# Attention and a mixture of experts on one core: the router's choice through PSUM, a small DMA descriptor memory, and a new order of work on every engine

## The chip, the cores and the metric

The kernel runs on one core of a Trainium2 chip. Five engines share the core's on-chip memory and run their own instruction streams: PE (TensorE, matmuls), DVE (VectorE), ACT (ScalarE), POOL (GpSimd) and SP (SyncE, which here only issues DMA transfers). The metric is the device time of one execution in microseconds; less is better.

## The reference, cut to what matters

```python
x = x + _L0_xattn_ref(_layernorm(x), ctx_1024, ctx_1024)     # x, ctx_1024: (16, 256, 256) f32: 4096 tokens of 256
x = x + _L0_ffn_ref(_layernorm(x), gate_w, gate_b, w1, b1, w2, b2)

# attention within one token: its 16 heads (16 values each) attend to the 16 heads of the same token of ctx
qh, kh, vh = [z.reshape(B, S, 16, 16) for z in (q, k, v)]
scores = jnp.einsum('bsqd,bskd->bsqk', qh, kh) / 4, causal over the heads
out = jnp.einsum('bsqk,bskd->bsqd', softmax(scores), vh)

# router and experts: 8 experts, each token goes to the one with the largest logit
top1 = jnp.argmax(xf @ gate_w.T + gate_b, axis=-1)
for e in range(8):
    h = relu(xf @ w1[e].T + b1[e])        # 256 -> 1024
    y = h @ w2[e].T + b2[e]               # 1024 -> 256
    out = out + jnp.where((top1 == e)[:, None], y, 0)
```

## The kernel before, in words

**Attention** goes in 16 chunks of 256 tokens (`NC`, in the code `i`). Of each chunk the queries are normalized on DVE (L974, L977, with the mean and deviation spread over the partitions by a PE product with `sel`, L1387), and queries, keys and values are split into a high and a low f16 half: the high one on ACT (L786, L794, L802), the rest on POOL (L1282, L1289, L1296). Small DMAs lay queries and values out as block diagonals in `arena` (L601, L603, L607; five of eight from SP's queue, three from ACT's). PE then makes the scores (L1396 the mask and L1403, 96 small products), DVE, ACT and POOL the softmax (L985 to L1000, L849, L1304), PE turns it (L1420) and multiplies by the values (L1433, 96 products), and DVE adds the residual (L1012).

**The router** works on groups of 4 chunks (`NG` = 4 groups, `g`). PE turns the group's output (L1445, in four steps) and makes the logits in the PSUM bank `lg_ps` (L1459, in four steps of four heads, 8 matmul rows each); DVE normalizes (L1020 to L1030, POOL's power L1321 between) and chooses: the generator `choose` in L1033 to L1094 is a chain of 15 small DVE steps per group that ends with `slot_i`, each row's place in a list sorted by expert. POOL then scatters the group's rows to DRAM (`sorted_rows`, L1340, 8 indirect DMAs). Three stages of a plan (L1113 to L1179) say which tile of 128 sorted rows belongs to which expert. The first 9 tiles need groups 0 and 1, the next 8 also group 2, the last 22 all four.

**The experts** work on 39 tiles of 128 rows: SP fetches a tile (L747), ACT and DVE normalize and split it (L871, L877, L1193), a DMA turns it (L767), PE makes the hidden layer (`ups`, L1506, 8 steps of 6 products), DVE, ACT and DVE its bias, relu and split (L1203, L886, L1214), PE the second layer (`downs`, L1522 and L1523, 8 steps of 2 products), DVE the result (L1228) and POOL stores it by an indirect DMA (L1366). The weights of the 8 experts are loaded (L660, L672, L679, L685) and split on ACT (L863) and DVE (L1186) while attention runs; the last of them land after it.

**The order.** On each engine the work is a set of generators, one for each kind of step. `weave` merges them by the table `TIMES`: every step has a number there, and an engine issues its steps in the order of these numbers. Nothing waits for a number; only their order counts, and each engine works strictly in that order, SP's DMA issues too. What an instruction needs is guarded by semaphore waits in front of it.

## Time and profile before

| | before |
|---|---|
| median of 3 runs | 467.47 us (467.33 to 468.16) |
| span of the profiled execution, first to last instruction | 462.9 us |
| what lies around the span, by the median | 4.6 us |
| PE busy | 384.6 us, 83% |
| DVE busy | 339.8 us, 73% |
| POOL busy | 207.6 us, 45% |
| ACT busy | 181.1 us, 39% |

The profile has one execution. Its own time as a run is not listed apart; the median less the span is what lies around it. A busy PE is not a PE at its peak, since its matmuls are pipelined and their ends modelled: a stretch of matmuls is best measured from the start of one group to the start of the next. Each row of the timeline merges neighbouring instructions of one kind.

### The profile page before, as it was taken

What the parts mean: (1) busy time and instruction counts of PE and PEld (TensorE: products, weight loads), DVE (VectorE), ACT (ScalarE), POOL (GpSimd) and SP (SyncE); (2) the same over time, 40 slices, a digit from 0 to 9 for tenths busy, and PEclk for the clock granted to TensorE, in tenths of its full rate; (3) what the DMA queues carried; (4) which work ended last, traced back from release to release, by engine and by line L of the source; (5) the groups of instructions that cost most, each with busy time, mean ns of one, the idle gap of its engine ahead of it and who ended that gap; (6) DMA issues with size and microseconds to landing.
All of it is one profiled execution on the core that took longest, in us unless ns stands there. A gap on an engine that the chain in (4) does not pass through costs nothing.

```text
span 462.9 us, 16301 instructions
## 1 busy us (share of the span) xinstructions
PE 384.6 (83%) x5889; PEld 328.5 (71%) x5889; DVE 339.8 (73%) x777; ACT 181.1 (39%) x317; POOL 207.6 (45%) x213
## 2 busy tenths in 40 slices
PE   0126878996798969895699999898999999999991
PEld 0026767996698869894688877676788888787870
DVE  8789799789882875378676987596867677766761
ACT  2344446454542523143353433243443434434320
POOL 8536444635673548643342354743333233233321
PEclk9999999955555555565589999999999999999998
DMA  7999989889778675667552544757543443434310
GB/s 264 417 254 236 264 220 260 260 188 240 200 161 218 159 160 112 180 141 219 125 143 67 107 98 106 186 139 184 106 94 99 95 108 90 104 84 106 100 29 0
DMA packets 125802, 73.17 MB, mean 158 GB/s; under 512 B 99229, under 2 KB 110238, under 8 KB 125216
## 3 DMA queue, kind: packets, MB, share of 16 engines
q1 hardware_dynamic: 96336, 60.46, 50.6%
q0 software_dynamic: 3408, 8.46, 5.0%
q10 hardware_dynamic: 25984, 3.21, 4.9%
q8 instruction: 52, 0.85, 0.7%
q14 instruction: 22, 0.18, 0.1%
HBM read 48.28 MB, written 11.24 MB: 129 GB/s over the span
## 4 chain that ended last, share of the span: by engine, by line
PE 58%; DVE 12%; issue 8%; SPq 7%; POOL 6%; DMA 5%; ACT 2%; POOLq 0%; DVEq 0%; ACTq 0%
PE s_ps L1506 19%; PE at_ps L1522 7%; PE pv_ps L1522 6%; PE s_ps L1403 6%; PE pv_ps L1433 5%; PE lg_ps L1459 4%; DMA arena<-qv_hl 3%; PE at_ps L1523 3%; PE pv_ps L1523 3%; SPq L601 3%; PE tr_ps L1445 2%; DVE arena L1186 2%; PE at_ps L1420 2%; POOL sorted_rows L1340 1%; POOL qv_hl L1296 1%
## 5 line engine op out<-in xcount | busy, mean ns | idle before, releaser
L1506 PEld LDWEIGHTS s_ps<-arena 128*128 x1872 | 131.9, 99 | 43.4 <-issue 4.9
L1506 PE MATMUL s_ps<-arena 128*128 128x128 f16 x1872 | 157.0, 221 | 2.8 <-issue 1.2
L1203 DVE SCALAR_TENSOR_TENSOR arena<-arena,s_ps 128x512 f32<-128x512 f32 x78 | 53.5, 685 | 32.5 <-PE s_ps L1506 21.1
L1433 PE MATMUL pv_ps<-a_hl,arena 128*128 128x16 f16 x1536 | 54.6, 180 | 17.1 <-DMA arena<-qv_hl 12.3
L1433 PEld LDWEIGHTS pv_ps<-a_hl,arena 128*128 128x128 f16 x1536 | 53.3, 118 | 20.7 <-DMA arena<-qv_hl 16.7
L1366 POOL DMA_INDIRECT result<-arena x39 | 38.9, 996 | 64.4 <-DVE arena L1228 60.3
L1403 PEld LDWEIGHTS s_ps<-k_hl,arena 128*128 128x128 f16 x1536 | 54.5, 118 | 15.4 <-DMA arena<-qv_hl 10.6
L1522 PE MATMUL at_ps<-arena,k_in 128*128 x160 | 60.3, 379 | 2.8 <-DVE k_hl L1214 2.8
L1359 POOL TENSOR_TENSOR arena<-arena 128x256 f32<-128x256 f32 x39 | 29.5, 756 | 73.4 <-DMA arena<-b 73.3
L1403 PE MATMUL s_ps<-k_hl,arena 128*128 128x16 f16 x1536 | 54.2, 180 | 9.7 <-DMA arena<-qv_hl 9.7
L1522 PE MATMUL pv_ps<-arena,x_in 128*128 x152 | 57.6, 379 | 0.0
L886 ACT ACTIVATE k_in<-arena 128x512 f16<-128x512 f32 x40 | 25.2, 629 | 60.5 <-DVE arena L1203 49.2
L1186 DVE SCALAR_TENSOR_TENSOR arena<-arena 128x512 f16<-128x512 f32 x56 | 47.7, 871 | 1.1 <-ACT arena L863 1.1
L863 ACT ACTIVATE arena<-arena 128x512 f16<-128x512 f32 x56 | 33.5, 623 | 33.3 <-issue 12.1
L886 ACT ACTIVATE x_in<-arena 128x512 f16<-128x512 f32 x38 | 23.9, 630 | 56.5 <-DVE arena L1203 42.0
L1523 PE MATMUL at_ps<-arena,k_hl 128*128 x160 | 43.6, 272 | 0.3 <-issue 0.3
L1523 PE MATMUL pv_ps<-arena,x_in 128*128 x152 | 41.4, 272 | 0.0
L1340 POOL DMA_INDIRECT sorted_rows<-pay,slot_i x32 | 33.2, 1037 | 15.2 <-issue 7.7
L1214 DVE SCALAR_TENSOR_TENSOR k_hl<-arena,k_in 128x512 f16<-128x512 f32 x40 | 27.4, 686 | 13.4 <-ACT k_in L886 13.0
L1282 POOL TENSOR_TENSOR qv_hl<-x_in,qv_hl 128x512 f16<-128x512 f32 x16 | 22.1, 1383 | 33.6 <-ACT qv_hl L786 33.6
L1214 DVE SCALAR_TENSOR_TENSOR x_in<-arena,x_in 128x512 f16<-128x512 f32 x38 | 27.0, 710 | 10.2 <-ACT x_in L886 9.4
L1459 PE MATMUL lg_ps<-gate_bd,o_sb 128*128 128x64 f32 x128 | 29.8, 408 | 2.3 <-DVE o_sb L1012 2.3
(141 smaller groups left out, 589.9 us busy)
## 6 DMA issues: line engine op xcount, KB each, us to landing
arena<-w SPq DMA_DIRECT2D x28, 512.0 KB, 5.1
arena<-sorted_rows SPq DMA_DIRECT2D x39, 130.0 KB, 2.2
arena<-b SPq DMA_DIRECT2D x39, 128.0 KB
arena<-qv_hl SPq DMA_DIRECT2D x70, 64.0 KB
k_in<-k_t SPq DMA_DIRECT2D x16, 256.0 KB
arena<-x SPq DMA_DIRECT2D x4, 1024.0 KB, 10.6
x_in<-x_t SPq DMA_DIRECT2D x16, 256.0 KB, 5.0
v_in<-v_t SPq DMA_DIRECT2D x16, 256.0 KB
```

The lines of the kernel that those rows point to most:

```text
L886: eng.activation(h_hi[j % 2][:, c * HALF:(c + 1) * HALF], h_in[:, c], ACT.Relu).then_inc(s_h_hi, 1)
L1186: eng.scalar_tensor_tensor(out=lo, in0=src, scalar=W_SCALE, in1=hi, op0=ALU.mult, op1=ALU.subtract).then_inc(s_w_lo, 1)
L1203: eng.scalar_tensor_tensor(out=h_in[:, c].rearrange("p (k t) -> p k t", t=P), in0=bias, scalar=W_SCALE, in1=h_ps[c][:].rearrange("p (k t) ...
L1214: eng.scalar_tensor_tensor(out=h_lo[j % 2][:, cols], in0=h_in[:, c], scalar=0.0, in1=h_hi[j % 2][:, cols], op0=ALU.max, op1=ALU.subtract). ...
L1340: eng.indirect_dma_start(out=sorted_rows, out_offset=bass.IndirectOffsetOnAxis(ap=slot_i[:, b:b + 1], axis=0), in_=pay[:, b, :], in_offset ...
L1366: eng.indirect_dma_start(out=out, out_offset=bass.IndirectOffsetOnAxis(ap=rows[:, r, :].bitcast(I32)[:, D + 2:D + 3], axis=0), in_=rows[:, ...
L1403: m = eng.matmul(s[:, n], q_bd[i % 2][:, n // 2, :, n % 2, q], k_hl[:, n, k, :], start=False, stop=(n, q) == (BLK - 1, 1))
L1433: m = eng.matmul(o[:, n], v_bd[i][:, n // 2, :, n % 2, v], a_hl[:, n, a, :], start=(n, a, v) == (0, 0, 0), stop=(n, v) == (BLK - 1, 1))
L1459: m = eng.matmul(LG, o_sb[:, :, h], gate_bd[:, h].rearrange("p b e -> p (b e)"), start=h == 0, stop=h == HEADS - 1)
L1506: k = eng.matmul(o, weights_of(j, w + k_ * H + n * P, P), xt[:, j % XB, a + k_], start=(k_, w, a) == (0, HI_1, 0), stop=k_ == KD - 1 and w ...
L1522: eng.matmul(y[:], h_hi[j % 2][:, n * P:(n + 1) * P], weights_of(j, at, 2 * D), start=n == 0, stop=False)
L1523: k = eng.matmul(y[:, 0:D], h_lo[j % 2][:, n * P:(n + 1) * P], weights_of(j, at, D), start=False, stop=n == KH - 1)
```

## The change

Four things change.

1. The DVE step that copies `turn_of` (0 or 1) into the selection matrix `sel` becomes a product of `turn_of` with itself, with the same result.
2. In `choose`, the values that go from step to step (`gate_sum`, `top`, `seen_now`, `slot_f` and two of the three parts of `route`, now `terms`) move from the on-chip memory SBUF to free columns of the PSUM bank that holds the logits. Nine of the 15 steps of a group now read such a value from PSUM that they read from SBUF before. With it the waits change a little: the first step now waits for the group's logits, and PE's logits of a group wait until the whole choice of the group before is done (`4 * g` in place of `4 * g - 3`).
3. The memory for the descriptors of POOL's indirect DMAs is 2048 bytes in each partition; it was the default, 16384.
4. All numbers of `TIMES` are new, on all five engines.

```diff
+        SMALL = 2 * G * E + E
+        gate_sum, seen_now = lg_bank[:, SMALL:SMALL + E], lg_bank[:, SMALL + E:SMALL + 2 * E]
+        slot_f = lg_bank[:, SMALL + 2 * E:SMALL + 2 * E + G]
+        top = lg_bank[:, SMALL + 2 * E + G:SMALL + 2 * E + 3 * G].rearrange("p (n g) -> p n g", n=2)
+        TERMS = SMALL + 2 * E + 3 * G
+        terms = [lg_bank[:, TERMS + n * G * E:TERMS + (n + 1) * G * E].rearrange("p (g e) -> p g e", g=G) for n in range(2)]
...
-                eng.tensor_copy(sel[:], turn_of[:].unsqueeze(2).to_broadcast([P, 8, HD])).then_inc(s_select, 1)
+                eng.tensor_tensor(sel[:], turn_of[:].unsqueeze(2).to_broadcast([P, 8, HD]),
+                                  turn_of[:].unsqueeze(2).to_broadcast([P, 8, HD]), ALU.mult).then_inc(s_select, 1)
...
-                    eng.tensor_tensor(v[1], pay[:, :, D:D + 1].to_broadcast([P, G, E]),
-                                      gate_sum[:].unsqueeze(1).to_broadcast([P, G, E]), ALU.mult).then_inc(s_hot, 1)
+                    dve.wait_ge(s_logits, g + 1)
+                    eng.tensor_tensor(terms[1], pay[:, :, D:D + 1].to_broadcast([P, G, E]),
+                                      gate_sum.unsqueeze(1).to_broadcast([P, G, E]), ALU.mult).then_inc(s_hot, 1)
...
-                    eng.tensor_tensor(v[2], v[1], first_wins[:].unsqueeze(1).to_broadcast([P, G, E]),
+                    eng.tensor_tensor(v[2], terms[1], first_wins[:].unsqueeze(1).to_broadcast([P, G, E]),
...
-                    eng.tensor_copy(slot_i[:], slot_f[:]).then_inc(s_slot, 1)
+                    eng.tensor_copy(slot_i[:], slot_f).then_inc(s_slot, 1)
...
-                            pe.wait_ge(s_slot, 4 * g - 3)
+                            pe.wait_ge(s_slot, 4 * g)
+                            pe.wait_ge(s_gate_sum, 1)
...
-    nc = bacc.Bacc("TRN2", target_bir_lowering=False, num_devices=1)
+    nc = bacc.Bacc("TRN2", target_bir_lowering=False, num_devices=1, dynamic_dma_scratch_size=2048)
```

Of the table `TIMES` for PE, the entries of the 16 blocks `outputs` (L1433):

```diff
-            4080, 5360, 6397, 7412, 8674, 9702, 10730, 11795, 13001, 14139, 15167, 16208, 17375, 18811, 19366,
-            20338
+            4389, 5561, 6655, 7647, 9125, 10442, 11475, 12493, 13929, 15219, 16293, 17303, 18710, 20275,
+            20842, 21744
```

Other entries of it for PE that the prediction uses (they are plain numbers that set the order):

| entry | before | after |
|---|---|---|
| `scores`, 6th, 7th, 11th, 15th of 16 | 7729, 9340, 13801, 17692 | 7964, 9878, 14859, 19027 |
| `ups`, first | 20827 | 22061 |
| `downs`, first and last | 21656, 42770 | 23468, 44089 |
| distance of `downs` from tile to tile in the last 20 tiles (8 steps) | 528 | 524 |
| usual distance from a step of `gates` (4 heads) to PE's next step | 85 | 186 |
| smallest distance from a block of `scores` to PE's next step | 338 | 359 |
| POOL: smallest distance from a scatter to POOL's next step | 96 | 135 |

Three places in the order follow. The first is DVE's beginning. `arena` at L940 is the raw input, of which the mean and deviation are taken, and at L1186 a piece of weights. Before:

```order
L898 MEMSET arena 128x4096
L901 TENSOR_REDUCE turn_of<-ident 128x8
L903 TENSOR_REDUCE unit_of<-ident 128x16
L906 TENSOR_REDUCE owner<-ident 128x8
L907 COPY sel<-turn_of 128x128
L940 BN_STATS xbn<-arena 128x6 x8
L1186 SCALAR_TENSOR_TENSOR arena<-arena 128x512
L945 BN_AGGR xbn<-xbn 128x2 x4
```

After (line numbers are those of the changed kernel):

```order
L909 MEMSET arena 128x4096
L952 BN_STATS xbn<-arena 128x6 x6
L1198 SCALAR_TENSOR_TENSOR arena<-arena 128x512
L952 BN_STATS xbn<-arena 128x6 x2
L957 BN_AGGR xbn<-xbn 128x2 x2
L912 TENSOR_REDUCE turn_of<-ident 128x8
L914 TENSOR_REDUCE unit_of<-ident 128x16
L917 TENSOR_REDUCE owner<-ident 128x8
L918 TENSOR_TENSOR sel<-turn_of 128x128
```

The step on `sel` moved from ahead of the statistics of the input to behind them.

The second is PE where attention ends. `pv_ps` is the last block of `outputs`, `lg_ps` with `gate_bd` a step of the last group's logits, `packed` the plan, `s_ps<-arena` the first tile's `ups`. Before:

```order
L1433 MATMUL pv_ps<-a_hl,arena 128x16 x96
L1459 MATMUL lg_ps<-gate_bd,o_sb 128x64 x4
L1484 TENSOR_LOAD packed
...
L1506 MATMUL s_ps<-arena 128x128 x2
...
L1459 MATMUL lg_ps<-gate_bd,o_sb 128x64 x4
...
L1445 MATMUL tr_ps<-ident,o_sb 128x128 x4
```

After:

```order
L1445 MATMUL pv_ps<-a_hl,arena 128x16 x96
L1497 TENSOR_LOAD packed
...
L1519 MATMUL s_ps<-arena 128x128 x2
...
L1472 MATMUL lg_ps<-gate_bd,o_sb 128x64 x4
```

The first step of the last group's logits moved from straight behind the last block of attention to behind all eight `ups` steps of the first tile; before, the second such step stood behind five of them.

The third is POOL at the second group's scatters; `k_hl` is the low half of a chunk's keys, the two rows `qv_hl` those of its queries and values. Before:

```order
L1340 DMA sorted_rows<-pay,slot_i 35840x260
L1282 TENSOR_TENSOR qv_hl<-x_in,qv_hl 128x512
L1340 DMA sorted_rows<-pay,slot_i 35840x260 x3
L1289 TENSOR_TENSOR k_hl<-k_in,k_hl 128x32x16
L1340 DMA sorted_rows<-pay,slot_i 35840x260 x3
L1296 TENSOR_TENSOR qv_hl<-v_in,qv_hl 128x512
```

After:

```order
L1352 DMA sorted_rows<-pay,slot_i 35840x260 x2
L1316 TENSOR_TENSOR a_sb<-a_sb,inverse 128x512
L1294 TENSOR_TENSOR qv_hl<-x_in,qv_hl 128x512
L1352 DMA sorted_rows<-pay,slot_i 35840x260 x6
L1301 TENSOR_TENSOR k_hl<-k_in,k_hl 128x32x16
L1308 TENSOR_TENSOR qv_hl<-v_in,qv_hl 128x512
```

The keys' step moved behind the last scatter of the group; the values' step stands behind all eight in both.

## Rows read from the trace of the kernel before

**Rows 1.** The page: TensorE's granted clock in tenths, in 40 equal slices of the span.

```profile
PEclk9999999955555555565589999999999999999998
```

**Rows 2.** Windows: stretch, us, busy time of each engine (x instructions), PEclk, DMA share, GB/s.

```profile
0.00:130.00 130.00, 83.77 (x1796) 76.67 (x1797) 111.63 (x266) 57.71 (x97) 71.47 (x71) 0.85 0.89 254
130.00:230.00 100.00, 82.60 (x1556) 77.74 (x1554) 65.08 (x165) 36.42 (x61) 50.99 (x48) 0.52 0.68 159
...
330.00:463.00 133.00, 123.48 (x1474) 97.97 (x1471) 87.66 (x162) 48.01 (x88) 41.26 (x48) 0.99 0.35 84
```

**Rows 3.** Timeline of DVE and POOL at the start: start us, us, engine, line, operation.

```profile
5.67 5.11 DVE L907 COPY sel<-turn_of 128x128 f32<-128x128 f32 x1
...
7.20 3.50 POOL L1268 MEMSET arena<- 128x4096 f32 x1
```

**Rows 4.** Timeline of PE: blocks of scores, and a piece of the second group's logits.

```profile
77.53 0.59 PE L1396 MATMUL s_ps<-mask_k,mask_q 128*128 128x512 bf16 x1
...
96.92 0.63 PE L1396 MATMUL s_ps<-mask_k,mask_q 128*128 128x512 bf16 x1
100.58 3.35 PE L1433 MATMUL pv_ps<-a_hl,arena 128*128 128x16 f16 x96
...
134.76 3.55 PE L1459 MATMUL lg_ps<-gate_bd,o_sb 128*128 128x64 f32 x16
138.11 1.06 PE L1445 MATMUL tr_ps<-ident,o_sb 128*128 128x128 f32 x4
...
193.92 0.59 PE L1396 MATMUL s_ps<-mask_k,mask_q 128*128 128x512 bf16 x1
```

**Rows 5.** Timeline of PE from attention's last block to the first tile.

```profile
222.85 3.35 PE L1433 MATMUL pv_ps<-a_hl,arena 128*128 128x16 f16 x96 [1.29 <-DMA arena<-qv_hl]
227.91 2.00 PE L1459 MATMUL lg_ps<-gate_bd,o_sb 128*128 128x64 f32 x8 [1.71 <-DVE o_sb L1012]
229.70 3.41 PE L1506 MATMUL s_ps<-arena 128*128 128x128 f16 x30
232.90 1.87 PE L1459 MATMUL lg_ps<-gate_bd,o_sb 128*128 128x64 f32 x8
```

**Rows 6.** Timeline of PE, from one `downs` step to the next, and the last ones.

```profile
254.37 0.38 PE L1522 MATMUL at_ps<-arena,k_in 128*128 x1
255.03 0.38 PE L1522 MATMUL at_ps<-arena,k_in 128*128 x1
...
453.67 0.38 PE L1522 MATMUL at_ps<-arena,k_in 128*128 x1
```

**Rows 7.** Timeline: a scatter of the second group, the keys behind it, PE's next scores.

```profile
186.29 0.98 POOL L1340 DMA_INDIRECT sorted_rows<-pay,slot_i  x1 [0.30 <-issue]
187.27 1.19 POOL L1289 TENSOR_TENSOR k_hl<-k_in,k_hl 128x512 f16<-128x512 f32 x1
...
194.29 3.38 PE L1403 MATMUL s_ps<-k_hl,arena 128*128 128x16 f16 x96
```

**Rows 8.** Groups by line: busy us, mean ns of one, idle before and its releaser.

```profile
L1186 DVE SCALAR_TENSOR_TENSOR arena<-arena 128x512 f16<-128x512 f32 x56 | 47.7, 871 | 1.1 <-ACT arena L863 1.1
L1048 DVE TENSOR_TENSOR route<-lg_ps,pay 128x64 f32<-128x64 f32 x4 | 0.9, 213 | 0.0
L1051 DVE TENSOR_TENSOR route<-route 128x64 f32<-128x64 f32 x4 | 0.9, 224 | 0.1
```

**Rows 9.** Timeline of DVE and POOL where a DVE step ends with a POOL step.

```profile
129.15 2.31 DVE L1186 SCALAR_TENSOR_TENSOR arena<-arena 128x512 f16<-128x512 f32 x1
129.82 1.08 POOL L1304 TENSOR_TENSOR a_sb<-a_sb,inverse 128x512 f32<-128x512 f32 x1
```

**Rows 10.** The last weights: timeline of ACT and DVE.

```profile
231.19 0.63 ACT L863 ACTIVATE arena<-x_in 128x512 f16<-128x512 f32 x1 [6.25 <-DMA x_in<-w]
231.85 0.69 DVE L1186 SCALAR_TENSOR_TENSOR arena<-x_in,arena 128x512 f16<-128x512 f32 x1 [3.40 <-issue]
```

**Rows 11.** The page: DMA issues, with the median us from issue to landing.

```profile
result<-arena POOLq DMA_INDIRECT x39, 3.1
```

More of the change, by code:

```diff
@@ L61 @@
+        "spread": (
[6 rows of a table added]
+        ),
+        "fill": (28734, 28890, 28996, 29220, 29376, 29912, 29968, 30418),
+        "fetch": (
[3 rows of a table added]
+        ),
+        "load_biases": (
[6 rows of a table added]
         ),
         "turn_rows": (
[3 rows of a table removed]
-        ),
-        "load_biases": (
[6 rows of a table removed]
-        ),
-        "fill": (26178, 26598, 26787, 27144, 27672, 28200, 28295, 28792),
[3 rows of a table added]
+        ),
     },
     "ACT": {
-        "weights": (
[5 rows of a table removed]
+        "spread_first_queries": (2163, 2332, 2573, 2633, 2803, 3309, 3440, 3613),
+        "spread": (
[4 rows of a table added]
+        ),
+        "queries": (
+            1940, 2447, 3369, 4123, 5776, 6312, 7546, 8195, 10134, 10679, 11944, 13588, 15065, 15811,
+            16856, 17867
@@ L138 @@
+        "outputs": (
+            5338, 6347, 7324, 8139, 10802, 11734, 12357, 12922, 15991, 16386, 17314, 17720, 20518,
+            21066, 22296, 22355
+        ),
+        "layer_norms": (
[6 rows of a table added]
+        ),
+        "choose": (
[5 rows of a table added]
+        ),
+        "counts": (28004,),
+        "plans": (
[5 rows of a table added]
         ),
         "weights": (
[5 rows of a table removed]
-        ),
-        "spreads": (1615, 4826, 9226, 13513),
[5 rows of a table added]
+        ),
+        "expert_inputs": (
[3 rows of a table added]
+        ),
+        "hiddens": (
[6 rows of a table added]
+        ),
+        "rests": (
[6 rows of a table added]
+        ),
+        "results": (
[6 rows of a table added]
+        ),
+    },
@@ L147 @@
+    "POOL": {
+        "constants": (0, 759, 862),
+        "zeros": (59, 409),
+        "statistics": (1349, 2786, 5421, 8940),
         "queries": (
-            1735, 1800, 1923, 2180, 2870, 3047, 3595, 3718, 5310, 5375, 5793, 5947, 6988, 7052, 7111, 7415,
-            9395, 9512, 9840, 9910, 10595, 10973, 11424, 12161, 13738, 13802, 14287, 14453, 14800, 15354, 16254,
-            16621
-        ),
-        "softmax": (
[6 rows of a table removed]
+            2025, 2532, 3454, 4505, 5861, 6462, 7631, 8528, 10219, 11009, 12672, 14053, 15150, 15896,
+            16941, 17985
+        ),
+        "keys": (
+            2291, 3885, 4740, 5585, 6326, 7760, 8412, 10347, 11347, 12557, 14388, 15533, 16222, 17211,
+            18924, 19765
+        ),
+        "values": (
+            1650, 4375, 5701, 6741, 7881, 9166, 10528, 11583, 12936, 14259, 15278, 16378, 17452, 19039,
+            20000, 20837
+        ),
+        "weights_of_softmax": (
+            3779, 4855, 6078, 7135, 8011, 9492, 10903, 12046, 13083, 13901, 15751, 16562, 17879, 19585,
+            20336, 21324
+        ),
+        "tables": (2951,),
+        "layer_norms": (10657, 16668, 21020, 26363),
+        "row_tails": (9296, 14504, 19738, 24925),
+        "scatters": (
+            12152, 12287, 12422, 12801, 13189, 13324, 13459, 13594, 17609, 17744, 18114, 18249, 18384,
+            18519, 18654, 18789, 22126, 22261, 22396, 22531, 22666, 23081, 23216, 23351, 28422, 28557,
+            28692, 28827, 28962, 29304, 29511, 29781
+        ),
+        "skipped_rows": (28107,),
+        "residuals": (
[3 rows of a table added]
+        ),
+        "stores": (
[3 rows of a table added]
+        ),
+    },
@@ L159 @@
+    "PE": {
+        "statistics": (1602, 5463, 9793, 14774),
+        "gate_columns": (1688,),
+        "scores": (
+            1731, 3980, 5056, 5878, 6972, 7964, 9878, 10759, 11792, 12809, 14859, 15536, 16763, 17620,
+            19027, 19916
+        ),
+        "turned": (
+            3894, 4970, 6238, 7332, 8681, 9628, 11119, 12161, 13198, 14331, 15975, 16677, 18166, 19744,
+            20592, 21438
         ),
         "outputs": (
-            5246, 6929, 7474, 7751, 10069, 11032, 11817, 12326, 14571, 15283, 16563, 16680, 19068, 19573, 20571,
```

176 lines of the change are left out of this document (58 added, 118 removed), and 289 rows, old and new, of the table TIMES.

## The prediction

> **What bounds the kernel now.** I read the page first, then windows by stage, then PE's timeline, and last the waits around the places where PE stands still. The first 130 us are attention with the weights loading and being split: DVE is busy 111.6 of 130 us and the DMA share is 0.89, PE only 83.8 us [rows 2]. From 130 to 230 us no engine is full: PE 82.6 of 100 us, DVE 65.1, DMA 0.68; the time goes into hand-overs between engines in the order the code gives them. From 330 us on PE is busy 123.5 of 133 us [rows 2], and its last matmul comes at 454: one step of a tile, 6 products of `ups` and 2 of `downs`, takes 255.03 − 254.37 = 0.66 us, a tile 8 × 0.66 = 5.28 us, and 39 tiles 206 us [rows 6]. So the end is set by two things: when attention's last block leaves PE, 222.85 + 3.20 = 226.05 us (3.35 by its record, less some 0.15 that overlaps what follows), and how little PE idles from there on.
>
> From 226.05 to the last product, 453.67 + 0.33 = 454.0 [rows 6], are 228.0 us. PE's work in it is 206 us of tiles, four steps of logits at (138.11 − 134.76) / 2 = 1.68 us, so 6.7 [rows 4], and some 2 us of transposes and counts: 214.7. 13.3 us are lost there, by waits and by a slow start: the first 30 products take 232.90 − 229.70 = 3.20 us, 107 ns each [rows 5]; later a step's six share 0.66 us less some 0.33 for the two of `downs` (0.38 by their record, with its overlap), 55 ns each. The first 30 run while the granted clock still stands at five tenths, the level of 1.2 GHz [rows 1]. The rest of the span, 462.9 − 454.0 = 8.9 us, is the last tile's way out; nothing in the change touches it.
>
> **The new order**, the main part. A step's number in the table acts only through the order, and none of my times is taken from it alone. But the numbers also say what durations the order was laid out for, and the trace can grade that, 10 ns a unit (528 units a tile against 5.28 us). The table before says 77.3 us for the sixth scores, the trace 77.53; then 93.4 and 96.92; 176.9 and 193.92 for the fifteenth [rows 4]; 203.4 and 222.85 for the last block of `outputs` [rows 5]. The order was made for a chip that is 19.5 us faster by then. Where from: a step of logits is given 0.85 us and takes 1.68, 12 of them in this stretch make 10.0 us; a block of scores gets 3.38 and takes 100.58 − 96.92 = 3.66 [rows 4], 15 make 4.2; a scatter gets 0.96 to 0.97 and takes 0.98 + 0.30 = 1.28 [rows 7], 24 make 7.4. That is 21.6 us against the 19.5. The new table gives these 1.86, 3.59 and 1.35 us: near the rows, the logits even 0.18 too long. An order laid out for durations that are true puts the right step next, one laid out for wrong ones makes engines wait for steps that the table thought done.
>
> What it is worth, first up to attention's end. The new table puts the last block of `outputs` at 217.4. The first numbers it shows are later than what the trace already does (sixth scores 79.6 against 77.53, seventh 98.8 against 96.92), and the fifteenth earlier (190.3 against 193.92). With 1 us for the start, my choice, since the table starts at 0 and the chip does not, and 2 us for what no table holds, of the size of the 2.1 by which the sum above misses, the block comes at 220.5: **2.3 us earlier**. The bounds: 217.4 + 1 says 4.4 us earlier; if the early delay of 2.1 + 1 us is kept and nothing is caught up, 3 us later.
>
> Second, behind attention. The old table itself leaves PE idle there: 427.7 + 0.33 − (203.4 + 3.17) = 221.5 us for 39 × 5.28 + 4 × 0.85 + 2 + 1.4 = 212.7 us of work, 8.8 us idle; the chip added 4.5 to reach 13.3. The new one: 440.9 + 0.33 − (217.4 + 3.17) = 220.7 us for 39 × 5.24 + 4 × 1.86 + 2 + 1.4 = 215.2 us, 5.5 us idle. Where it comes from shows in the second piece of order: before, PE stands 1.71 us for the last o_sb, does the logits, then 30 products of the first tile [rows 5]; after, the tile's 48 products come first and the logits fill the wait for the first hidden layer. Against it: 18 more products at the slow level, 18 × 52 ns = 0.9 us. With the chip's own 4.5 again: 13.3 − (5.5 + 4.5 + 0.9) = **2.4 us less**. Bounds: 0, if the last weights hold the first `downs` as they do now, and 5.
>
> **The port holds.** The copy into `sel` takes 5.11 us and ends at 10.78, with POOL's second memset, 7.20 + 3.50 = 10.70 [rows 3]. Alone it would take some 0.2. A piece of weights at 129.15 takes 2.31 us and ends 0.56 behind a POOL step that ran to 130.90; over 56 of these the mean is 871 ns where one takes 0.69 undisturbed [rows 10], (871 − 690) × 56 = 10 us of DVE in all [rows 8, 9]. The Trainium skill, "SBUF — State Buffer", section "Who interferes with whom", says why: an f32 copy within SBUF, and a step with two SBUF inputs while POOL reads SBUF, wait for the whole POOL instruction; a product escapes POOL's memset, which only writes, and a value in PSUM escapes altogether. The trace agrees so far.
>
> The product frees up to 4.9 us of DVE at the start. But it is also moved behind the statistics, whose input is still landing, and the first queries' DMAs then meet a stretch with a DMA share of 0.89 [rows 2]. I take 0.8 us at PE's end, bounds 0 and 2.5. The PSUM values spare `choose` a few holds of 0.4 to 1.1 us, on the path only when a scatter waits: 0.2 us, bounds 0 and 1. What hides the rest is the load on the DMA engines; if that cover is gone, up to the 2.5 appear.
>
> Against this stands a rule of the same notes: "VectorE: DVE Perf Modes", section "The TRN2 errata", gives a PSUM source 62 cycles more than SBUF. By it nine steps in four groups would cost 36 × 65 ns = 2.3 us of DVE, not all on the path. The rows show no such cost: 213 ns with `lg_ps` as input, 224 ns without, same size [rows 8]. I take 0.
>
> **The waits.** PE's logits now wait for the whole choice of the group before. Behind them stand transposes and scores. In both orders a group's logits stand well behind: the tightest is the second to third group, where scatter work has begun before the logits start. 0; at most one step, 0.3 us.
>
> **The descriptor memory.** No row prices it. An indirect DMA lands 3.1 us after its issue [rows 11], and they come each 1.28 us [rows 7], so some three are under way; an eighth of the memory would have to be too small for three. Below: nothing, no gain either, since POOL's step writes as many descriptors. Above: each scatter waits for the one before, 3.1 in place of 1.28 us, 1.8 × 8 = 15 us a group, of which some 10 could reach the path. I take 0, the nearer end by the three under way.
>
> **Scatters and keys**, the third piece: the keys now stand behind three more scatters, 3 × 1.28 = 3.8 us later. Before, they end at 188.46 and the scores start at 194.29 [rows 7], a cover of 5.8 us. 0, with 2 us left of the cover.
>
> **Sum:** 2.3 + 2.4 + 0.8 + 0.2 = 5.7 us off a span of 462.9: 457.2. The median stands 4.6 above the span: 461.8 us. Half of the 0.8 may already be in the 2.3; I say 462.
>
> **Rivals.**
> 1. The new order runs nearly as its table says: attention 4.4 us earlier, 5 us less idle, start 2.5. 462.9 − 11.9, so 455.6 us. For it: the graded durations. Against it: 4.5 us that every table misses. Chance 0.15.
> 2. The gain is eaten where it is made: the last weights arrive by a DMA at 231.2 and are split from 231.85 on [rows 10], and only then the first hidden layer can go on. If the new order loads them no earlier, an earlier end of attention buys nothing: 467.5, within 0.9. For it: the loads wait for `x_in` and `a_sb`, free only at attention's end. Against: that end itself moves. Chance 0.10.
> 3. Slower: attention ends later. The early delay of 3 us stays and DVE, which is nearly full up to 130 us, loses again what the table leaves out, the 10 us of port holds, half of them on the path: last `outputs` block at 222.85 + 3 + 5 = 231, less the 2.4 behind it, so +5.6: 473. It is slower from where that block starts after 225.5. Chance 0.20.
> 4. The descriptor memory stalls the scatters: +5 to +10, 470 to 477. Chance 0.05.
> My forecast, a gain of 2 to 9 us: 0.50.
>
> **How the numbers follow.** This kernel's runs tell 0.2%, 0.9 us, from no change. Faster: 0.50 + 0.15 and a little of rival 2 = 0.67; same 0.09; slower 0.24. The range leaves out the best half of rival 1 and the worst of 3 and 4: 455 to 471. The likeliest case alone: 458.5 to 465.5.
>
> **What would show it.** `sel` under 0.5 us; the last block of attention on PE between 218 and 222; the first `ups` straight behind it with no idle of 1.7 us; the last matmul near 448.5; tiles still 5.28 us; scatters still 1.28 us apart. Wrong it would be if that block starts after 225, if the distance from it to the last matmul is not under 231 − 2 us, or if scatters stand more than 1.4 us apart.

## The result, and the profile after

The changed kernel is slower. In the first measurement it took 470.74 us in the median of 20 runs (466.84 to 474.83), the kernel before, beside it, 465.50 us (462.06 to 469.30): a ratio of 1.0101, 95% interval 1.0078 to 1.0124. The forecast was 462.

The three runs shown ahead of the prediction, 467.33 to 468.16 us, are among those 20, and they lie above the median of them all. The kernel before took 465.0 to 465.6 us in three of the jobs (groups of runs that were measured side by side) and 470.9 to 471.3 in the two others, so times are compared within a job only. The medians take in all runs, the ratios leave out those more than 1.5% above the fastest run of the same kernel.

The page of the kernel after, and its windows (columns as in [rows 2]):

```profile
span 470.9 us, 16308 instructions
PEclk9999999965555755565598999998999999999999
```

```profile
0.00:130.00 130.00, 78.59 (x1642) 71.10 (x1642) 100.80 (x259) 56.23 (x93) 67.21 (x66) 0.87 0.87 240
130.00:230.00 100.00, 82.09 (x1618) 76.83 (x1619) 61.18 (x161) 37.67 (x63) 52.59 (x49) 0.55 0.70 173
...
330.00:471.00 141.00, 134.35 (x1602) 106.60 (x1600) 95.86 (x179) 52.62 (x97) 44.10 (x51) 0.99 0.38 88
```

DVE did less in the first 130 us, 100.80 us against 111.63, and so did PE, 78.59 against 83.77 [rows 2]: the work was not taken away but came later. The timeline of PE shows where. The second and third scores before, then rows of the kernel after:

```profile
37.14 0.63 PE L1396 MATMUL s_ps<-mask_k,mask_q 128*128 128x512 bf16 x1
...
47.47 0.63 PE L1396 MATMUL s_ps<-mask_k,mask_q 128*128 128x512 bf16 x1
```

```profile
39.58 0.63 PE L1408 MATMUL s_ps<-mask_k,mask_q 128*128 128x512 bf16 x1
...
52.39 0.63 PE L1408 MATMUL s_ps<-mask_k,mask_q 128*128 128x512 bf16 x1
...
82.48 0.59 PE L1408 MATMUL s_ps<-mask_k,mask_q 128*128 128x512 bf16 x1
...
229.33 3.34 PE L1445 MATMUL pv_ps<-a_hl,arena 128*128 128x16 f16 x96 [2.56 <-DMA arena<-qv_hl]
233.41 4.41 PE L1519 MATMUL s_ps<-arena 128*128 128x128 f16 x48 [0.74 <-issue]
...
465.87 0.38 PE L1535 MATMUL at_ps<-arena,k_in 128*128 x1
```

The third scores come 4.9 us later than before, so most of the delay is there early. The sixth scores come at 82.48 where they came at 77.53 [rows 4], the last block of attention at 229.33 in place of 222.85 [rows 5]: 6.5 us later, where I had said 2.3 earlier. The first `ups` follow with an idle of 0.74 us and all 48 in one piece, as forecast. From that block's start to the last `downs` it is 465.87 − 229.33 = 236.5 us, before 453.67 − 222.85 = 230.8: 5.7 more, where I had said 2.4 less. That makes 12.2 us for PE's end, but the span is only 470.9 − 462.9 = 8.0 us longer. The rest is in the tail, which I had called untouched. The last store on POOL, before and after:

```profile
455.87 0.97 POOL L1366 DMA_INDIRECT result<-arena  x1 [2.14 <-DVE arena L1228]
```

```profile
468.07 0.97 POOL L1378 DMA_INDIRECT result<-arena  x1 [2.14 <-DVE arena L1240]
```

After, it is 470.9 − 469.04 = 1.9 us from its end to the end of the span. Before, its end was at 456.84, and the span went on for 6.1 us to its end at 462.9.

A profile shows a single execution; that of the changed kernel was 2.0 us above the median. So the sizes below are taken from groups of runs where they can be.

### The profile page after: what moved, and what is told of

The parts are those of the page before. It is cut to its first block, busy times and chain, and to the rows that moved or that the text cites. A ratio compares the mean times of both kernels' runs of the same rounds, so it can differ in the third digit from the quotient of the medians.

```text
span 470.9 us, 16308 instructions
## 1 busy us (share of the span) xinstructions
PE 387.6 (82%) x5889; PEld 328.9 (70%) x5889; DVE 329.0 (70%) x777; ACT 181.8 (39%) x317; POOL 210.1 (45%) x213
## 4 chain that ended last, share of the span: by engine, by line
PE 38%; DMA 18%; SPq 15%; POOL 10%; DVE 8%; issue 8%; ACT 3%; POOLq 0%; ACTq 0%; DVEq 0%
PE s_ps L1519 14%; DMA arena<-qv_hl 8%; SPq L612 6%; PE at_ps L1535 5%; PE pv_ps L1445 5%; PE pv_ps L1535 4%; DMA arena<-sorted_rows 3%; DMA arena<-b 3%; POOL sorted_rows L1352 3%; PE at_ps L1536 3%; PE pv_ps L1536 2%; PE s_ps L1415 2%; DVE arena L1198 2%; SPq L778 2%; POOL qv_hl L1294 2%
## 5 line engine op out<-in xcount | busy, mean ns | idle before, releaser
L1519 PEld LDWEIGHTS s_ps<-arena 128*128 x1872 | 130.1, 99 | 42.6 <-issue 8.7
L1519 PE MATMUL s_ps<-arena 128*128 128x128 f16 x1872 | 152.5, 221 | 5.6 <-DMA arena<-arena 2.9
L1198 DVE SCALAR_TENSOR_TENSOR arena<-arena 128x512 f16<-128x512 f32 x56 | 45.1, 818 | 8.9 <-ACT arena L874 8.9
L1352 POOL DMA_INDIRECT sorted_rows<-pay,slot_i x32 | 35.5, 1109 | 19.1 <-issue 9.6
L882 ACT ACTIVATE arena<-arena 128x256 f32<-128x256 f32 x39 | 23.1, 593 | 24.9 <-DMA arena<-sorted_rows 21.6
```

Of the source, the lines that this page charges most:

```text
L1198: eng.scalar_tensor_tensor(out=lo, in0=src, scalar=W_SCALE, in1=hi, op0=ALU.mult, op1=ALU.subtract).then_inc(s_w_lo, 1)
L1352: eng.indirect_dma_start(out=sorted_rows, out_offset=bass.IndirectOffsetOnAxis(ap=slot_i[:, b:b + 1], axis=0), in_=pay[:, b, :], in_offset ...
L1519: k = eng.matmul(o, weights_of(j, w + k_ * H + n * P, P), xt[:, j % XB, a + k_], start=(k_, w, a) == (0, HI_1, 0), stop=k_ == KD - 1 and w ...
```

## The experiments

Ratios are to the kernel before in the same job, with their 95% intervals. "Block" is the start of the last block of attention on PE, "tiles" the time from the first to the last product of `downs`, "tail" that from the end of POOL's last store to the end of the span, all three from one profile each. That execution is within 2.7 us of its kernel's median, but for e13 (3.4 us below) and e2 (470.89 us, 5.9 above, so that the block and the tiles of e2 say little).

| run | median, before beside it | ratio | block | tiles | tail |
|---|---|---|---|---|---|
| the change | 470.74, 465.50 | 1.0101 (1.0078 to 1.0124) | 229.33 | 220.7 | 1.9 |
| e1 order only | 480.94, 470.93 | 1.0188 (1.0143 to 1.0233) | 229.78 | 221.4 | 6.1 |
| e2 code only | 464.99, 470.93 | 0.9841 (0.9799 to 0.9882) | 224.94 | 216.4 | 1.8 |
| e3 descriptor memory only | 465.67, 470.93 | 0.9875 (0.9834 to 0.9915) | 223.17 | 219.2 | 1.8 |
| e4 new order on DVE only | 483.18, 470.93 | 1.0251 (1.0208 to 1.0294) | 224.28 | 225.4 | 6.1 |
| e5 the change again | 476.39, 471.25 | 1.0040 (0.9990 to 1.0090) | 231.19 | 222.1 | 1.8 |
| e6 old order up to the block | 469.40, 471.25 | 0.9960 (0.9929 to 0.9990) | 221.55 | 221.7 | 1.8 |
| e7 new order up to the block | 473.60, 471.25 | 1.0041 (1.0009 to 1.0072) | 229.37 | 222.5 | 1.8 |
| e8 old order up to the 4th scores | 470.76, 471.25 | 0.9976 (0.9941 to 1.0011) | 226.18 | 223.8 | 1.8 |
| e9 scatters together | 470.79, 465.62 | 1.0110 (1.0072 to 1.0148) | 228.49 | 220.0 | 1.9 |
| e10 ACT's start | 470.33, 465.62 | 1.0073 (1.0030 to 1.0117) | 227.62 | 219.4 | 1.9 |
| e11 product for `sel` only | 466.03, 465.62 | 0.9991 (0.9945 to 1.0037) | 222.55 | 213.2 | 6.1 |
| e12 8192 bytes | 462.97, 465.62 | 0.9935 (0.9897 to 0.9972) | 223.38 | 214.3 | 3.1 |
| e13 fills spread | 471.57, 465.05 | 1.0164 (1.0115 to 1.0212) | 227.90 | 217.7 | 1.8 |
| e14 no port hold | 469.97, 465.05 | 1.0119 (1.0070 to 1.0169) | 228.80 | 218.0 | 1.9 |
| e15 three mended | 471.09, 465.05 | 1.0128 (1.0075 to 1.0181) | 227.49 | 220.4 | 1.9 |
| e16 PSUM only | 464.53, 465.05 | 0.9991 (0.9960 to 1.0023) | 224.61 | 214.7 | 6.1 |

The ratio of e5 rests on four of its twelve runs, since one of them, at 469.05, was far below the others, which begin at 473.91. By the medians it is 1.011, as in the first measurement. For e6 to e8 I compare medians, and say beside it what the ratios give.

### Which of the four parts costs

**e1**, the kernel before with the new table, and **e2**, the new code with the old table:

```diff
 TIMES = {
...
         "keys": (
-            1045, 3438, 4282, 5131, 6267, 7295,
+            2223, 3673, 4671, 5436, 6258, 7492,
...
```

> The kernel before with the new table of numbers on all five engines and nothing else changed. Theory A (the new order is what costs): the whole slowdown is here, a ratio of 1.008 to 1.012, near 470.5 us; the second block of scores comes at about 39.6 us on PE in place of 37.1, the third at 52.4 in place of 47.5, the last block of attention at 228 to 230. Rival B (the small descriptor memory costs): ratio 1.000 or less, and the third block of scores is at 47 to 49. Rival C (the values in PSUM and the longer wait of the logits cost): as B.

> The kernel before with the three other edits (product for sel, values of the choice in PSUM, descriptor memory of 2048 bytes) and the old table. Theory A: ratio 0.996 to 1.001; sel takes under 0.5 us, and PE's last block of attention moves by less than 1 us. Rivals B and C: ratio 1.006 to 1.012, and it shows behind the first scatter, at about 130 us, not before it.

The order alone costs 10.0 us, the code alone gives 5.9. Rivals B and C fall: the three edits of the code together cost nothing, and neither do the memory (e3) and the values in PSUM (e16) by themselves, below. Both runs miss theory A's numbers: e1 has 1.0188, not 1.008 to 1.012, since what the code gives back is missing in it, and e2 has 0.9841, not 0.996 to 1.001. The block of e2 is also 2.1 us later than before and not within 1, in a profile 5.9 us above the median. 10.0 − 5.9 = 4.1, against 5.2 and 5.1 measured for the whole in its two jobs. A lower granted clock is not what the order costs: its mean is 0.842 to 0.853 in the six runs of e1 and 0.837 to 0.854 in those of the kernel before beside them.

**e3**, the descriptor memory alone, and **e12**, a size between:

```diff
-    nc = bacc.Bacc("TRN2", target_bir_lowering=False, num_devices=1)
+    nc = bacc.Bacc("TRN2", target_bir_lowering=False, num_devices=1, dynamic_dma_scratch_size=2048)
```

> The kernel before with a descriptor memory of 2048 bytes in each partition and nothing else changed. Theory A: ratio 0.999 to 1.001, scatters 1.28 us apart as before. Rival B: 1.006 or more, with scatters further apart than 1.4 us. A side question: the last store of the profile before takes 6.1 us from POOL's end to the end of the span, the changed kernel's 1.9; if the memory's size does that, it is 1.9 here, and if it is chance, either.

> The kernel before with a descriptor memory of 8192 bytes in each partition in place of 16384. From the end of POOL's last store to the end of the span it was 6.1 us with 16384 bytes (7.5 and 8.9 by the last product) and 1.9 with 2048. If that time grows evenly with the size, it is 3.6 to 3.9 us here and the ratio 0.995; if it is a step between two ways of ending, 1.9 or 6.1.

2048 bytes give 5.3 us where theory A said none, and 8192 bytes give 2.7. The ends of the profiles say where. The span and POOL's last row, of e3, e12 and e11 (2048, 8192 and 16384 bytes):

```profile
span 464.9 us, 16301 instructions
462.09 0.97 POOL L1366 DMA_INDIRECT result<-arena  x1 [2.14 <-DVE arena L1228]
```

```profile
span 460.6 us, 16301 instructions
456.55 0.97 POOL L1366 DMA_INDIRECT result<-arena  x1 [2.14 <-DVE arena L1228]
```

```profile
span 461.7 us, 16301 instructions
454.59 0.97 POOL L1367 DMA_INDIRECT result<-arena  x1 [2.14 <-DVE arena L1229]
```

The tail is 464.9 − 463.06 = 1.8 us, 460.6 − 457.52 = 3.1 us and 461.7 − 455.56 = 6.1 us. It is the same in every run of the table with the same memory, whatever the order. Neither expectation for 8192 bytes fits: 3.1 us is not the 3.6 to 3.9 of an even growth (it grows by 1.2 us over the first 6144 bytes and by 3.0 over the next 8192), and not a step. One reading is that the end of the program does something of 3.0 us for 8192 bytes beside the landing of the last store, which alone needs 1.8; that is an estimate from three points and not shown. The scatters in e3 stand 1.28 us apart as before, so no scatter is seen to wait for room in a memory of 2048 bytes.

**e11**, the product alone:

```diff
-                eng.tensor_copy(sel[:], turn_of[:].unsqueeze(2).to_broadcast([P, 8, HD])).then_inc(s_select, 1)
+                eng.tensor_tensor(sel[:], turn_of[:].unsqueeze(2).to_broadcast([P, 8, HD]),
+                                  turn_of[:].unsqueeze(2).to_broadcast([P, 8, HD]), ALU.mult).then_inc(s_select, 1)
```

> The kernel before with the product for sel and nothing else. My prediction gave this edit 0.8 us, with 0 to 2.5 as bounds. If it holds: sel takes 0.3 us, the first block of scores comes 1 to 2 us earlier, the last block of attention 0 to 1 us, ratio 0.996 to 1.000. If a gain at the start is kept: 0.995.

```profile
5.67 0.28 DVE L907 TENSOR_TENSOR sel<-turn_of 128x128 f32<-128x128 f32 x1
...
14.91 0.63 PE L1397 MATMUL s_ps<-mask_k,mask_q 128*128 128x512 bf16 x1
...
36.58 0.63 PE L1397 MATMUL s_ps<-mask_k,mask_q 128*128 128x512 bf16 x1
...
222.55 3.37 PE L1434 MATMUL pv_ps<-a_hl,arena 128*128 128x16 f16 x96 [1.73 <-DMA arena<-qv_hl]
```

4.8 us are freed; 2.1 are left at the first scores (17.01 before), 0.6 at the second (37.14), 0.3 at the last block, and in the time nothing that can be told from zero. The gain runs out on the way. The interval, 2 us to each side, also holds the 0.8 us of the prediction. I had named the load on the DMA engines as what hides it; no run tested that.

**e16**, the values in PSUM alone: the diff of `choose` above, with the copy for `sel` and the memory as before.

> The kernel before with the values of the choice in PSUM and the longer wait of the logits, old table, copy for sel and descriptor memory of 16384 bytes. My prediction gave this 0.2 us less, with bounds of 0 and 1, and a page's rule 2.3 us more of DVE time. By the first the ratio is 0.998 to 1.000, by the second 1.001 to 1.005.

The ratio, 0.9991, fits both readings' edges; the rows decide. The group of `slot_i` before, and the groups of the choice in the changed kernel (columns as in [rows 8]):

```profile
L1094 DVE CAST slot_i<-slot_f 128x8 int32<-128x8 f32 x4 | 2.0, 505 | 0.0
```

```profile
L1061 DVE TENSOR_TENSOR route<-lg_ps,pay 128x64 f32<-128x64 f32 x4 | 0.8, 201 | 0.0
L1064 DVE TENSOR_TENSOR lg_ps<-route,lg_ps 128x64 f32<-128x64 f32 x4 | 0.9, 224 | 0.1
L1106 DVE CAST slot_i<-lg_ps 128x8 int32<-128x8 f32 x4 | 0.7, 164 | 0.1
```

The first of the choice's steps shown read PSUM before as well, 201 ns after and 213 before. The second read SBUF alone before and reads PSUM now, and it takes 224 ns in both [rows 8]. The 62 more cycles of the Trainium skill, "VectorE: DVE Perf Modes", section "The TRN2 errata", are not seen in these steps. And `slot_i`, 505 ns on average before, takes 164 here and 156 in e16: with its value in PSUM it no longer waits. That the port hold goes away is shown, that it is worth time is not.

### Where the order costs

**e4**, the old order with the new one on DVE alone.

```diff
     "DVE": {
-        "constants": (170, 509, 1405, 2045, 4500),
+        "constants": (0, 1124, 1753, 1960, 4732),
...
```

> The kernel before with the new numbers for DVE alone, the other four engines in the old order. Theory A with DVE at its root (it puts the first chunk's row maximum behind the next chunk's two normalizing steps, and the deviation of the second part of the input 2.3 us later): the second block of scores comes at about 39.5 us, and the ratio is 1.004 to 1.012. If the root lies in another engine's order, the ratio is within 1.002 and the second block of scores stays at 37.

The second scores come at 36.35 us, not late: my first theory of the start falls, and the ratio, 1.0251, lies outside both readings. DVE's order puts the row maximum behind the next chunk's steps here too, and here it costs nothing at the second scores. Most of the 12.3 us that this run loses lie behind attention (the block comes 1.4 us late, then the first `downs` 20.3 us behind it in place of 16.8, and the tiles take 225.4 us), where DVE's order no longer fits the others'; it says nothing on the new table as a whole.

**e5 to e8** cut the table in time. Each takes the numbers of one table up to a step and those of the other behind it, moved by the difference of the two at that step. All four have the new code, and e5 is the changed kernel.

```python
# p: a step's number in the early table, q: its number in the late one; E, L: those of the step at the cut
number = p if p < E else q - L + E      # raised where needed, so that no step passes the one before it
# e6: early old, late new, cut at the last outputs (E, L = 20338, 21744); e7: the reverse
# e8: early old, late new, cut at the fourth scores (E, L = 5677, 5878)
```

> The changed kernel once more, as the base of the three runs beside it. Ratio 1.010 as before if the first measurement holds, in 1.006 to 1.014; last block of attention at 229.3 us within 1, no POOL or DMA work in the last 1.9 us of the span.

> The changed kernel with the old numbers for every step that stood ahead of the last block of outputs, and the new ones behind it. Theory A (the cost of the new order lies in attention, and most of it in its first 50 us): last block at 223 to 224 us and a ratio 0.013 below the changed kernel's, 0.997. Rival D (it lies behind attention): last block at 223, but the time no more than 2 us under the changed kernel's.

> The reverse: the new numbers up to the last block of outputs, the old ones behind it. Theory A: last block at 229.3 us, and within 2 us of the changed kernel. Rival D: last block at 229.3, and the time 3 us or more under the changed kernel's.

> The changed kernel with the old numbers for the steps ahead of the fourth block of scores (number 5677, some 57 us) and the new ones from there on. Theory A: second and third block of scores at 37 and 47.5 us in place of 39.6 and 52.4, the last block of attention 4 to 5 us earlier than the changed kernel's, at 225 us, and the ratio 0.009 below it. Rival E (each stretch of attention loses a little, so a good start is lost again): last block at 227 to 229 and the ratio within 0.004 of the changed kernel's.

e5 itself misses two of its expectations, with its block at 231.19 (229.3 within 1) and its ratio of 1.0040 (1.006 to 1.014). The block of e6 is earlier than the 223 to 224 expected, that of e8 1.2 us later than its 225. Against e5's median of 476.39 us, the old order in attention gives 7.0 us back (e6), the old one behind it 2.8 (e7), and the old one in the first 57 us alone 5.6 (e8). By the ratios, with the 1.0101 of the first measurement as base, it is 6.6, 2.8 and 5.9 us; with e5's own 1.0040, whose interval is 0.5% to each side, 3.8, nothing and 3.0. So theory A holds for the larger part: the order costs in attention, and most of it at the start. A cost behind attention, rival D, is less sure: e7's median is between what the two had said, and its tiles take 222.5 us although their numbers are the old ones. The last block of e6, the old order up to there, and that of e8:

```profile
221.55 3.36 PE L1208 MATMUL pv_ps<-a_hl,arena 128*128 128x16 f16 x96 [2.46 <-DMA arena<-qv_hl]
```

```profile
37.58 0.63 PE L1171 MATMUL s_ps<-mask_k,mask_q 128*128 128x512 bf16 x1
...
48.16 0.63 PE L1171 MATMUL s_ps<-mask_k,mask_q 128*128 128x512 bf16 x1
...
226.18 3.34 PE L1208 MATMUL pv_ps<-a_hl,arena 128*128 128x16 f16 x96 [2.88 <-DMA arena<-qv_hl]
```

The latter is 5.0 us before the changed kernel's in the same job (231.19) and 4.6 behind that of e6. So a good start is kept in part: e8 is 0.2 us behind the kernel before at the fourth scores and 3.1 at the sixteenth.

### Which step in it

Four late steps were found in the trace of the changed kernel and mended, each alone, and three of them together.

**e10**, ACT at the start. In the changed kernel:

```profile
22.85 0.62 ACT L805 CAST k_hl<-k_in 128x512 f16<-128x512 f32 x1 [2.68 <-POOL qv_hl L1294]
...
24.03 1.21 DVE L1198 SCALAR_TENSOR_TENSOR arena<-arena 128x512 f16<-128x512 f32 x1 [0.93 <-ACT arena L874]
25.33 1.74 DVE L1198 SCALAR_TENSOR_TENSOR arena<-arena 128x512 f16<-128x512 f32 x1
...
29.98 0.17 DVE L963 SCALAR_TENSOR_TENSOR xstat<-xbn,xstat 128x8 f32<-128x8 f32 x1 [1.76 <-POOL xstat L1287]
```

ACT's split of the first keys stands behind its wait for POOL's first queries, and its next weights stand behind that. DVE's weights wait for them (0.93 us), and then take 1.21 and 1.74 us beside steps of POOL where 0.65 is usual. The deviation of the next input stands behind those.

```diff
         "keys": (
-            2223, 3673,
+            790, 3673,
...
         "weights": (
-            730, 785, 2277, 2392,
+            730, 785, 1600, 1650,
```

> The changed kernel with three of ACT's numbers put ahead as before: the first keys between the first two pieces of weights and the spreading of the first queries, and the third and fourth piece of weights behind the first values. Theory H (ACT's new order is the root of the late start, since DVE's next piece of weights waits for ACT's, which waits behind POOL's first queries, and the second part of the deviation waits behind that piece): DVE's wait of 0.93 us for ACT at 24.0 is gone, the second block of scores comes at 37.0 to 38.3 us in place of 39.6, the third at 48 to 50.5 in place of 52.4, the ratio is 1.002 to 1.007. Rival: other orders (SP's loads, DVE's) carry it, and the blocks stay within 0.5 us.

```profile
28.40 0.17 DVE L963 SCALAR_TENSOR_TENSOR xstat<-xbn,xstat 128x8 f32<-128x8 f32 x1 [1.76 <-POOL xstat L1287]
...
37.99 0.63 PE L1408 MATMUL s_ps<-mask_k,mask_q 128*128 128x512 bf16 x1
...
51.35 0.63 PE L1408 MATMUL s_ps<-mask_k,mask_q 128*128 128x512 bf16 x1
```

The deviation comes 1.6 us earlier and the second scores with it, as expected. The third come only 1.0 us earlier and miss the expectation: something else is between. The ratio, 1.0073 (1.0030 to 1.0117), is just above its range too, and the median is 4.7 us above the kernel before, against 5.2 for the changed kernel.

**e14**, and what that is. The changed kernel on POOL and DVE at the second chunk's softmax:

```profile
48.45 2.98 POOL L1316 TENSOR_TENSOR a_sb<-a_sb,inverse 128x512 f32<-128x512 f32 x1
48.63 1.88 DVE L1198 SCALAR_TENSOR_TENSOR arena<-arena 128x512 f16<-128x512 f32 x3
51.48 1.11 PE L1432 MATMUL at_ps<-ident,a_sb 128*128 128x128 f32 x4 [4.17 <-POOL a_sb L1316]
```

POOL's product takes 2.98 us; its time is 1.06. It starts by its record 0.18 us before DVE's run of three pieces and ends 0.9 us behind it. PE waits for it.

```diff
-            981, 1236, 2347, 2483, 2587, 2968, 3063, 3124, 3543, 4020, 4149, 4294, 5003, 5064, 5125,
-            5216, 6191,
+            981, 1236, 2347, 2483, 2587, 2968, 3063, 3124, 3543, 4020, 4149, 4294, 5217, 5218, 5219,
+            5220, 6191,
```

> The changed kernel with DVE's three pieces of weights at 48.6 us moved behind the four aggregates that follow them, so that POOL's step on the second chunk's weights of the softmax starts before them. Theory J (POOL's 2.98 us there, 1.06 elsewhere, are a wait for DVE's run of three on the shared port): POOL's step takes 1.0 to 1.4 us, the third block of scores comes at 50.3 to 50.9 us in place of 52.4, the ratio falls by 0.001 to 0.004. Rival: POOL's step stays at 3 us, because something else holds it.

```profile
48.00 3.41 DVE L1198 SCALAR_TENSOR_TENSOR arena<-arena 128x512 f16<-128x512 f32 x3
48.76 1.50 POOL L1316 TENSOR_TENSOR a_sb<-a_sb,inverse 128x512 f32<-128x512 f32 x1
...
51.22 0.63 PE L1408 MATMUL s_ps<-mask_k,mask_q 128*128 128x512 bf16 x1
```

Now POOL has 1.50 us and DVE's three pieces 3.41: the wait changed sides. The cause is as theory J said, though POOL's step is 0.1 us above its range and the third scores stay 0.3 us short of theirs. The time doesn't follow: 1.0119, where a fall by 0.001 to 0.004 was expected.

**e9** and **e13**, behind attention. In the changed kernel two residual steps of POOL stand within the third group's scatters, and three fills on SP between a tile's fetch and its turn.

```diff
-            22801, 22873, 23486, 24813, 25664, 26082, 27274, 27502, 27828, 28035, 29097, 29439, 29916,
+            23352, 23353, 23486, 24813, 25664, 26082, 27274, 27502, 27828, 28035, 29097, 29439, 29916,
```

> The changed kernel with one thing put back: POOL does the third group's eight scatters without the first two residual steps between the fifth and the sixth. Theory F (these two steps hold the scatters up and through them ACT's copy of the last group's transposes and PE behind it): scatters done 3 us earlier, 14 to 15 us behind the start of the last block of attention in place of 17.6; ACT's first copy of the last group at 17 in place of 20; the time 1 to 3 us less than the changed kernel's, a ratio to the kernel before of 1.004 to 1.008. Rival G (the loss behind attention is spread over many places): the scatters move but the time doesn't, 1.009 to 1.012.

```diff
-        "fill": (28734, 28890, 28996, 29220, 29376, 29912, 29968, 30418),
+        "fill": (28272, 28677, 28734, 29091, 29376, 29558, 29912, 30418),
```

> The changed kernel with the eight fills on SP spread as before, never more than one between a fetch and the turn behind it (the new order has three there). Theory I (SP's new order holds the turned rows of tiles 10 to 14 back: 3 fills at 2.4 us each stand ahead of one turn): the distance from the first to the last product of the second layer, 220.0 us on average in the three runs with the new order on this kind of chip and 213.9 in the three with the old, falls to 215 to 217.5; the ratio is 0.999 to 1.005 in place of 1.010. Rival: contention of the transfers themselves; the distance stays above 219.

ACT's first copy of the last group, which waits for the scatters, is at 249.55 in the changed kernel, 20.2 us behind the block; in e9 it is at 246.23, 17.7 behind. The step moved as theory F said, and the time did not: rival G. In e13 the tiles take 217.7 us, just above the range of theory I, and the time is no better at all: the ratio of 1.0164 is rather worse than the changed kernel's 1.0101. That profile was the fastest of six runs, 3.4 us under their median. Theory I is not borne out.

**e15**, the edits of e10, e13 and e14 together.

> The edits of the last two together with that of ACT's first keys and weights (the run on ACT's start). If the three causes are separate and add up: third block of scores at 49.5 us, last block of attention at 226, first to last product of the second layer 215 to 217.5, ratio 0.993 to 1.000. If a good start is lost again in attention: last block at 228 or later.

The third scores are at 50.02 and the block at 227.49, 1.8 us before the changed kernel's, of the 3 and more that were expected; the tiles take 220.4, where 215 to 217.5 were. The ratio is 1.0128. The three mends don't add up to anything in the time, of which 0.993 to 1.000 was expected. The changed kernel did not run again in the jobs of e9 to e15, so these five mended kernels stand against its first measurement, through the kernel before in each job.

## Why the prediction was wrong

**The new order, first half** (2.3 us earlier at attention's end) is the step that failed, with the wrong sign: 6.5 us later in the profile, 7.0 us of time in e6. It was worked out from the table's end, 217.4, plus 3 (which is 220.4 and 2.4 us, not 220.5 and 2.3). What the chip shows against the table: scores 1 and 2 at 17.32 and 39.58 (the table: 17.31 and 39.80), the third at 52.39 (50.56), the sixth at 82.48 (79.64), the last block at 229.33 (217.44). So 12 us are missed, not 3. The premise that failed is that an order laid out for truer durations puts the right step next. I had graded the old table only to find its misses. Its first six numbers for the scores are right to 0.6 us, five of them to 0.25: in that stretch the old order ran as laid out, and the new one leaves its table at the third block. The early 2.1 us that I saw in the numbers were not a matter of bookkeeping; they became 5.0 us on the chip (82.48 − 77.53).

**Second half** (2.4 us less behind attention): 5.7 more in the profile, 2.8 us of time in e7. The piece that I read in the order did what I said: the idle of 1.71 us is gone, and the first `downs` come 16.0 us behind the block in place of 16.8. But the tiles, which I had at 5.28 us each in both orders, take 220.7 in place of 214.2 us. In the runs on the kind of chip where the kernel before takes 465 us, four with the old order have 214.2, 213.2, 214.3 and 214.7, six with the new one or a mended one 220.7, 220.0, 219.4, 217.7, 218.0 and 220.4. On the other kind of chip the two orders are not told apart by their tiles: 216.4 and 219.2 in e2 and e3, but 222.5 in e7, with old numbers there, and 221.4 to 223.8 in the four with new ones. So that the tiles' loss comes from the order behind attention is not shown. The 5.28 us hold from tile 17 on; of the 6.5 us, 2.5 are lost in the first seven tiles and 4 from there to tile 16. PE after, in windows (columns as in [rows 2]):

```profile
318.00:323.00 5.00, 1.85 (x17) 0.96 (x14) 1.49 (x3) 1.54 (x3) 1.89 (x3) 0.90 0.74 179
323.00:328.00 5.00, 5.00 (x49) 3.89 (x47) 3.56 (x11) 2.26 (x4) 1.31 (x2) 0.75 0.57 135
328.00:333.00 5.00, 5.00 (x63) 4.02 (x61) 3.43 (x9) 0.73 (x2) 1.72 (x2) 1.00 1.10 227
```

PE is busy 1.85 of 5 us, and then the granted clock is 0.75 on average for a stretch in which it is busy throughout, before it is back at 1.00: this stand is paid again. The row that ends it:

```profile
321.56 0.63 PE L1519 MATMUL s_ps<-arena 128*128 128x128 f16 x6 [2.90 <-DMA arena<-arena]
```

Here a tile's turned rows come 2.90 us late.

**Port holds.** The rows did what was forecast: `sel` takes 0.28 us, `slot_i` 164 ns. DVE's pieces of weights, which none of the edits of the code touches, take 818 ns in place of 871:

```profile
L1198 DVE SCALAR_TENSOR_TENSOR arena<-arena 128x512 f16<-128x512 f32 x56 | 45.1, 818 | 8.9 <-ACT arena L874 8.9
```

The 0.8 + 0.2 us that I put on them are not seen in the time, nor ruled out: e11 and e16 give 0.9991 each, with intervals of 0.3 to 0.5% that hold zero and these sizes alike. Rival 3's mechanism, a table that leaves holds out, is seen in its reverse, POOL held by DVE, but mending that hold gave no time that could be told from noise (e14).

**The waits** and **the scatters and keys**: 0, and no run speaks against it; e16, with the longer wait of the logits, is at 0.9991 of the kernel before. No run moved the keys alone.

**The descriptor memory** at 0 was mis-sized: its gain was excluded by a reason, that POOL's step writes as many descriptors. That fits the scatters, 1.28 us apart in both, and says nothing on the end of the program. It is 4.2 us in the tail and 5.3 us in the median of e3. With it the tail's "nothing in the change touches it" falls. The two misses have opposite signs; with the order alone, without this gain, e1 is 2% slower.

**What lies around the span**, 4.6 us, was mis-sized as well. It was the median of three runs less a span from another execution. In every run of which both are known, the time is 1.8 to 2.0 us above the span. With that the same sum, 457.2, gives 459 and not 462. The three runs also made the noise look like 0.2%, while the 20 go from 462.06 to 469.30.

**Rival 3** is nearest to what came: it had the last block at 231 (229.33) and 473 us (470.74), and its first half, an early delay that stays, is what the rows show. I gave it 0.20. Its other half, 5 us of port holds, no run bears out. That the time came so near is luck, since it also kept the 2.4 us gain behind attention, where the profile has 5.7 more, and knew nothing of the 4.2 us in the tail. Its threshold, slower from where the block starts after 225.5, fails: in e8 it starts at 226.18, and e8 is not slower than the kernel before (0.9976). By the same luck 470.74 lies just inside the stated range, which ends at 471.

**Still open** is what in the order costs the time. That it is the order is shown (e1, e2), and that the larger part arises in attention, mostly at its start (e6, e8). The late steps that I found in attention and at the scatters were moved back by their mends, and no mend made the kernel faster by more than its interval, alone or with two others. The intervals of these runs reach 0.4 to 0.5% to each side, so 2 us could be hidden in any of them, but not the 5 to 10 us of the whole.

**A version that beats both** is e2: the three edits of the code with the old order, 0.984 of the kernel before. e3, the small descriptor memory alone, has 0.9875, which its interval does not tell from e2.

## What to carry to other kernels

An order laid out from truer durations is not thereby a better one. Look first where the old table and its trace agree to a few tenths of a microsecond: there the true durations had nothing to mend, and here the new order lost most in just that stretch. Cut two orders in time and join them, which shows in which stretch the cost lies; single mends of late steps, each right in its row, gave nothing that could be told from noise. And read the tail between the last store and the end of the span: a setting that seems to have nothing to do with it can set its length.

## What the runs showed of the hardware

- The memory for the descriptors of indirect DMAs has a price at the end of the program: 6.1 us from the last store's end to the span's with 16384 bytes, 3.1 with 8192, 1.8 to 1.9 with 2048, in all 18 profiles.
- The hold between DVE and POOL goes both ways: POOL's step, 1.06 us elsewhere, took 2.98 beside three DVE pieces issued back to back, and with DVE's pieces issued later in the order POOL's took 1.50 and the three 3.41 in place of 1.88. The Trainium skill, "SBUF — State Buffer", section "Who interferes with whom", says of the shared ports that they are an exclusive lock and that issue order, not op shape, decides who blocks. The trace agrees as to the hold, not plainly as to the order: POOL's record starts 0.18 us before DVE's first piece and ends 0.9 us behind the third, so it did not get in between the three either.
- The same program took 465 us in some jobs and 471 in others, and e3's tiles took 219.2 us where e12's, in the same order but with a descriptor memory of 8192 bytes, took 214.3.
